# First attention of a two-layer kernel: probabilities transposed by VectorE in 32x32 blocks instead of by TensorE

## The chip, the core and the metric

One Trainium2 chip, one of its NeuronCores. The metric is the device time of one execution in microseconds (us). The five engines are TensorE (PE; its weight loads are PEld), VectorE (DVE), ScalarE (ACT), GpSimd (POOL) and SyncE (SP); they run their own instruction streams and meet only at semaphores.

## The reference

Two layers over x of shape (128, 64, 128), each a cross-attention to a context (128, 64, 96) and a mixture of experts, both with gated residuals. The change is in the first attention alone, 16 heads of width 8, 64 queries and 64 keys per batch entry:

```python
q = (layernorm(x) @ wq + bq)   # 16 heads of 8
k = (ctx @ wk + bk); v = (ctx @ wv + bv)
scores = einsum('bhqd,bhkd->bhqk', q, k) / sqrt(8)
attn = softmax(scores, axis=-1)
out = einsum('bhqk,bhkd->bhqd', attn, v)
x = x + tanh(g_xattn[0]) * (out.reshape(B, S, 128) @ wo + bo)
```

## The kernel before

The kernel is one program of phases that follow each other: constants, first attention (`attention_of_layer0`), first mixture, second attention with routing, second mixture. In the first attention the work unit is a tile of 128 rows, two batch entries of 64; there are 64 tiles, in 16 groups of four. Each engine runs a function `step(t, u, g0)`, with u = t mod 8, in which every operation works on a tile some steps behind: tile t gets its scores, t-1 its maxima subtracted and its exponential, t-2 and t-3 the rest, t-4 the output projection and the update of X. `loop_steps` (lines 45 to 55) writes out the first eight steps, then a loop of eight steps that is run six times with one branch back per turn, then the last twelve. So PE's code for eight steps is one loop body. Nothing schedules but the written order on each engine and the semaphores.

In PE's step: scores of a tile (L619), eight float32 matmuls that contract 32 rows (a batch entry's half of the packed heads) and give 64 queries by 256 (four heads by 64 keys). A float32 matmul appears in the trace as two records. Queries lie on partitions. The row maxima, split in two bfloat16 parts and transposed (L693), are subtracted by a small matmul against `head_cols` (L629), contracting 32 rows for each of the two PSUM banks. The probabilities (`probs`, 128 queries by 16 heads x 64 keys) are transposed on PE in two halves of four 128x128 blocks into one PSUM bank (L646), and ScalarE copies each half to `probsT` (L541). P times V (L675) is 16 matmuls of 128 rows by 32 columns. VectorE sums the denominators (L385), takes reciprocals (L394) and widens them (L406); PE transposes the widened reciprocals (L662) and VectorE multiplies (L419). Line 642 is the output projection. `prepare` makes the next group's normalised rows, keys, queries and values, one of the four kinds per step (L585, L594, L600), through one PSUM bank `prep`; ScalarE copies them out (`evacuate`), VectorE half of the values (`v_odd`, L373); GpSimd spreads the keys over heads (L465).

```python
for s in range(2):
    last = pe.matmul(scores[(u + 1) % 2][:, s, :], rows[bass.ts(s, STRIP), :], c.head_cols[bass.ts(s, STRIP), :],
                     start=False, stop=True, skip_group_check=True)
```

Of the kernel before, what the change touches and what calls it, by code (L numbers as in the profile page):

```python
# [74 lines left out]
def load_constants(nc, sb, psum, sem, c, a, X, dispatch):  # L75
# [15 lines left out]
    c.head_cols_f = sb("head_cols_f", [2 * STRIP, HU * S], F32)  # L91
    c.head_cols = sb("head_cols", [2 * STRIP, HU * S], BF16)
# [38 lines left out]
    c.v_heads = [sb(f"v_heads{i}", [P, GB, HU, STRIP], F32) for i in range(2)]  # L131
    c.parts = sb("parts", [P, P], BF16)
# [13 lines left out]
    def spread(ap, n):  # L146
# [6 lines left out]
        (c.head_of_group[:], a["const_head_of_group"]), (c.head_cols_f[:], a["const_head_cols"]),  # L153
# [28 lines left out]
    with nc.Block() as block:  # L182
# [8 lines left out]
        @block.gpsimd  # L191
        def _(pool):
            pool.memset(c.parts[:], 0.0)
            pool.memset(c.minus_half[:], -0.5)

        @block.scalar
        def _(act):
            act.wait_ge(loads, 16 * len(now))
            act.activation(c.gates[:], c.gates_in[:], ACT.Tanh).then_inc(tanh_done, 1)

        @block.vector
        def _(dve):
# [4 lines left out]
            dve.tensor_copy(c.head_cols[:], c.head_cols_f[:])  # L207
# [55 lines left out]
def attention_of_layer0(nc, sb, psum, sem, c, a, X, dispatch):  # L263
# [14 lines left out]
    neg_max = sb("a_neg_max", [P, H], F32)  # L278


    parts = c.parts
    rows = sb("a_rows", [2 * STRIP, P], BF16)
    probs = [sb(f"a_probs{i}", [P, H * S], F32) for i in range(2)]
    probsT = [sb(f"a_probsT{i}", [P, HU, P], F32) for i in range(2)]
    denom = sb("a_denom", [P, H], F32)
    rec = sb("a_rec", [P, H], F32)
    wide_rec = [sb(f"a_wide_rec{i}", [P, H, DH], F32) for i in range(2)]
    heads_raw = sb("a_heads_raw", [P, P], F32)
    heads_outT = sb("a_heads_outT", [P, P], F32)

    scores = [psum(f"a_scores{i}", [P, 2, 512], F32) for i in range(2)]
    probsT_bank = psum("a_probsT_bank", [P, 512], F32)
    prep = psum("a_prep", [P, 512], F32)
    small = psum("a_small", [P, 512], F32)
    pv = psum("a_pv", [P, 2, P], F32)
    max_parts = parts[:, 0:2 * STRIP].rearrange("p (s a h) -> p s a h", s=2, h=HU)
    max_by_bank = neg_max[:].rearrange("p (s h) -> p s h", s=2)
    y = small[:, 0:D]
    rows_ps = small[:, D:D + P // 2].bitcast(BF16)
# [3 lines left out]
    prep_mm, prep_ev, v_odd_ev = sem("a_prep_mm"), sem("a_prep_ev"), sem("a_v_odd_ev")  # L303
    k_heads_ready = sem("a_k_heads")
    scores_mm, max_done, part1_done, parts_ready = sem("a_scores_mm"), sem("a_max"), sem("a_part1"), sem("a_parts")
# [1479 lines left out]
```

## Time and profile before

| | us |
|---|---|
| median of 3 runs | 1073.1 (1068.34 to 1078.13) |
| the profiled execution | 1074.11 |
| its span, first to last instruction | 1072.3 |
| PE busy | 829.9 (77%) |
| VectorE busy | 680.7 (63%) |
| ScalarE busy | 522.5 (49%) |
| GpSimd busy | 452.0 (42%) |

The first attention takes about the first 334 us of the span. Shares of the whole span mix phases with different limits; the rows below are of the first attention alone.

### The profile page before, as it was taken

Reading aid. Unit: us, or ns where it says so; the run is one execution under the profiler, and the core shown is the slowest. Engines: PE = TensorE matmul, PEld = TensorE weight load, DVE = VectorE, ACT = ScalarE, POOL = GpSimd, SP = SyncE. Lnnn points to the kernel's source line nnn. Section 1 sums busy time; section 2 is a strip of 40 time slices with the busy share of each in tenths; the row PEclk is TensorE's granted clock in tenths of the full one; section 3 lists DMA queues with packets and bytes.
Section 4 is the critical chain, followed back from the end, with each engine's and each line's share of the span. In section 5 each row is a group of like instructions: output and inputs, shape, how many; then the busy total and the mean of one; then the engine's idle time right before and its main releaser. Section 6 shows DMA issues by size and latency. Waiting matters only on the chain. (4 is left out here: it accounts for less than half of the span.)

```text
span 1072.3 us, 25830 instructions
## 1 busy us (share of the span) xinstructions
PE 829.9 (77%) x7905; PEld 607.8 (57%) x7905; DVE 680.7 (63%) x2651; ACT 522.5 (49%) x1115; POOL 452.0 (42%) x454
## 2 busy tenths in 40 slices
PE   2899999999985999996776776763388887887820
PEld 1466666666653566664554554543277776776720
DVE  3688988998895688875855464554244444444435
ACT  1577777777764455543543443442244344433400
POOL 1354544445430111101465655667355555555530
PEclk9999999999997899998966657765699999999965
DMA  4401010100000000002111111111222222222249
GB/s 116 121 20 37 17 34 17 34 17 25 11 2 2 1 0 0 0 2 72 36 48 41 48 40 42 43 38 46 82 76 77 70 73 76 71 70 69 71 154 345
DMA packets 64384, 57.47 MB, mean 54 GB/s; under 512 B 18453, under 2 KB 57901, under 8 KB 64333
## 3 DMA queue, kind: packets, MB, share of 16 engines
q1 hardware_dynamic: 46669, 34.28, 11.1%
q0 software_dynamic: 8640, 17.84, 4.7%
q10 hardware_dynamic: 9024, 4.73, 1.5%
q8 instruction: 25, 0.41, 0.2%
q14 instruction: 26, 0.21, 0.1%
HBM read 32.80 MB, written 24.02 MB: 53 GB/s over the span
## 5 line engine op out<-in xcount | busy, mean ns | idle before, releaser
L1596 POOL DMA_INDIRECT contributions<-d_y,d_token x142 | 135.9, 957 | 135.2 <-DVE d_y L1636 94.0
L1233 POOL DMA_INDIRECT sorted_rows<-r_send,r_slots x128 | 124.7, 974 | 51.4 <-issue 50.6
L1685 PE MATMUL d_u<-d_xT,d_w 128*128 128x256 f32 x284 | 80.6, 409 | 39.2 <-DVE d_xT L1617 21.5
L1656 ACT ACTIVATE d_silu<-d_u 128x512 f32<-128x512 f32 x71 | 42.4, 597 | 139.2 <-PE d_u L1685 88.1
L1617 DVE COPY d_xT<-d_tr 128x256 f32<-128x256 f32 x71 | 30.0, 423 | 120.7 <-PE d_tr L1693 57.5
L465 POOL TENSOR_SCALAR a_k_heads<-a_kT,head_of_group 128x512 f32<-128x512 f32 x60 | 92.9, 1566 | 2.7 <-ACT a_kT L510 2.7
L388 DVE TENSOR_REDUCE a_neg_max<-a_scores 128x16 f32<-128x1024 f32 x64 | 78.2, 1222 | 10.6 <-PE a_scores L619 9.1
L646 PE MATMUL a_probsT_bank<-ident,a_probs 128*128 128x128 f32 x512 | 80.5, 280 | 2.2 <-ACT a_probsT L541 0.3
L541 ACT COPY a_probsT<-a_probsT_bank 128x512 f32<-128x512 f32 x128 | 74.9, 585 | 11.3 <-PE a_probsT_bank L646 11.3
L534 ACT ACTIVATE a_probs<-a_scores 128x1024 f32<-128x1024 f32 x64 | 65.6, 1025 | 28.7 <-PE a_scores L629 28.6
L1685 PEld LDWEIGHTS d_u<-d_xT,d_w 128*128 128x128 f32 x284 | 50.7, 199 | 49.6 <-issue 21.5
L385 DVE TENSOR_REDUCE a_denom<-a_probs 128x16 f32<-128x1024 f32 x64 | 77.3, 1208 | 1.7 <-issue 1.2
L1685 PE MATMUL d_v<-d_xT,d_w 128*128 128x256 f32 x284 | 76.9, 395 | 0.0
L1704 PE MATMUL d_y_bank<-d_w,d_hidden 128*128 128x128 f32 x568 | 75.1, 275 | 0.8 <-DVE d_hidden L1625 0.8
L619 PE MATMUL a_scores<-a_k_heads,a_qT 32*64 32x256 f32 x1024 | 71.7, 395 | 2.8 <-issue 2.6
L1704 PEld LDWEIGHTS d_y_bank<-d_w,d_hidden 128*128 128x128 f32 x568 | 69.1, 192 | 1.1 <-DVE d_hidden L1625 1.0
L646 PEld LDWEIGHTS a_probsT_bank<-ident,a_probs 128*128 128x128 f32 x512 | 56.9, 141 | 17.8 <-issue 11.2
L1636 DVE TENSOR_SCALAR d_y<-d_y_bank,d_rows 128x128 f32<-128x128 f32 x142 | 43.0, 345 | 31.0 <-remote 26.3
L456 POOL TENSOR_TENSOR X<-X,out_bias 128x512 f32 (+1 forms) x16 | 20.6, 1285 | 98.8 <-ACT a_xn L497 98.8
L1685 PEld LDWEIGHTS d_v<-d_xT,d_w 128*128 128x128 f32 x284 | 56.9, 200 | 8.6
L66 POOL TENSOR_SCALAR b_rstd<-b_stats 128x4 f32<-128x4 f32 x16 | 3.7, 228 | 137.5 <-DVE b_stats L752 137.5
L1035 PE MATMUL b_h<-b_xnT,w 128*128 128x512 f32 x96 | 58.3, 694 | 0.0
(208 smaller groups left out, 1915.3 us busy)
## 6 DMA issues: line engine op xcount, KB each, us to landing
d_rows<-sorted_rows SPq DMA_DIRECT2D x71, 130.0 KB
d_pair<-contributions SPq DMA_DIRECT2D x16, 512.0 KB, 7.0
X<-in_x SPq DMA_DIRECT2D x16, 256.0 KB, 3.0
out_x<-X ACTq DMA_DIRECT2D x16, 256.0 KB, 7.4
ctxT<-in_ctx_T SPq DMA_DIRECT2D x16, 192.0 KB, 3.0
c_ctx<-in_ctx SPq DMA_DIRECT2D x16, 192.0 KB
contributions<-d_y,d_token POOLq DMA_INDIRECT x142
w<-in_L_ffn_W SPq DMA_DIRECT2D x2, 1024.0 KB
```

The lines of the kernel that those rows point to most:

```text
L385: dve.reduce_sum(denom[:], probs[u % 2][:].rearrange("p (h k) -> p h k", k=S), AX_X).then_inc(sum_done, 1)
L388: dve.tensor_reduce(neg_max[:], scores[u % 2][:].rearrange("p a (h k) -> p (a h) k", k=S), AX_X, ALU.max, negate=True).then_inc(max_done, 1)
L465: last = pool.tensor_scalar(keys_of_head(par, j), kT[:], c.head_of_group[:, j:j + 1], None, ALU.mult)
L534: act.activation(probs[(u + 1) % 2][:], scores[(u + 1) % 2][:].rearrange("p a n -> p (a n)"), ACT.Exp, scale=SCALE0).then_inc(exp_done, 1)
L541: act.copy(probsT[u % 2][:, half * HU // 2:(half + 1) * HU // 2, :].rearrange("p u q -> p (u q)"), probsT_bank[:]).then_inc(pT_ev, 1)
L619: last = pe.matmul(scores[u % 2][S * b:S * b + S, s, bass.ts(h, 4 * S)], qT[par][rows_in, h, tile, :], k_heads[par][rows_in, tile, h].rear ...
L646: last = pe.transpose(probsT_bank[:, bass.ts(k, P)], probs[u % 2][:, bass.ts(half * HU // 2 + k, P)], c.ident[:])
L1035: pe.matmul(h_bank[(C0 * par + k) % 2][:], c.w1_0[:, 2 * k:2 * k + 2, :].rearrange("d e h -> d (e h)"), xnT[par][:], start=True, stop=True ...
L1233: pool.indirect_dma_start(dispatch.rows, bass.IndirectOffsetOnAxis(ap=slots[par][:, k, j:j + 1], axis=0), send[par][k][:, j, :], None).the ...
L1596: pool.indirect_dma_start(dispatch.contributions, bass.IndirectOffsetOnAxis(ap=token[u % 2][:, h:h + 1], axis=0), shares[u % 2][:, h, :], ...
L1685: last = pe.matmul(bank[q][:, bass.ts(k, TP)], w12[q][:, i * HID1 + k * P:i * HID1 + k * P + P], xT[q][:], start=True, stop=True)
L1704: last = pe.matmul(y[q][:, bass.ts(h, D)], hidden[q][:, k, bass.ts(h, P)], w3[(u + 2) % 4][:, bass.ts(k, D)], start=(k == 0), stop=(k == K ...
```

## The change

Scores are computed so that a partition strip of 32 holds one block of 32 keys' worth of results: a strip is (batch entry, key block j), and within it 32 queries; the free side runs over head, query block i and 32 keys. VectorE then transposes all 32x32 blocks in place with one instruction (`dve.transpose`, 128x1024), and keys lie on partitions. For this the score matmuls become 32 of 32 rows by 32 columns by 128. Maxima: VectorE reduces over each strip of 32 keys, PE transposes that (float32) into the `prep` bank, VectorE takes the minimum over the two key blocks, copies it broadcast as bfloat16 and forms the rest, 32 partitions by 128 each; the subtraction contracts 64 rows for each bank, and `head_cols` is made on the chip from the identity by two ScalarE copies instead of being loaded. P times V becomes 32 matmuls of 64 rows by 32 columns by 64, and 32 more of the same form against ones give the denominators, already in the layout of the outputs. ScalarE takes the reciprocal as exp(-ln(denominator)) and VectorE multiplies. The order of `prepare` becomes keys, rows, queries, values, one per step; a table set with exp and ln is loaded at the start of the phase. Gone are the probability transposes on PE and their copies, the transpose of reciprocals, the denominator sum, the reciprocal, the widening and `v_odd`.

```diff
@@ VectorE's step, in its order @@
+                n = tile_now(t, 3)
+                if n is not None:
+                    dve.wait_ge(rec_step, 2 * n + 2)
...
+                    dve.tensor_tensor(heads_outT[:], rec[:], pv[:, :, 0:S], ALU.mult).then_inc(o_ready, 1)
+                n = tile_now(t, 2)
+                if n is not None:
+                    dve.wait_ge(exp_done, n + 1)
...
+                    dve.transpose(probsT[u % 2][:].rearrange("p h q -> p (h q)"),
+                                  probs[u % 2][:].rearrange("p h i k -> p (h i k)")).then_inc(probsT_ready, 1)
...
+                    dve.tensor_reduce(part_max[:], scores[u % 2][:].rearrange("p s (n k) -> p (s n) k", k=STRIP), AX_X,
+                                      ALU.max, negate=True).then_inc(part_max_done, 1)
...
+                    dve.wait_ge(part_max_mm, n + 1)
+                    dve.tensor_reduce(neg_max[:], part_maxT.rearrange("r (b j q) -> r b q j", b=2, j=2), AX_X,
+                                      ALU.min).then_inc(max_done, 1)
...
+                    dve.tensor_copy(rows[0:STRIP], both).then_inc(high_done, 1)
+                    dve.wait_ge(high_done, n + 1)
+                    dve.tensor_tensor(rows[STRIP:2 * STRIP], both, rows[0:STRIP], ALU.subtract).then_inc(rows_ready, 1)
@@ ScalarE's step @@
+                    act.wait_ge(pv_mm, n + 1)
+                    act.activation(log_denom[:], pv[:, :, S:2 * S], ACT.Ln).then_inc(rec_step, 1)
+                    act.wait_ge(rec_step, 2 * n + 1)
...
+                    act.activation(rec[:], log_denom[:], ACT.Exp, scale=-1.0).then_inc(rec_step, 1)
...
+            act.preload_act_table_set("natural_log_exp_and_others")
+            evacuate(0, 0, KEYS)
@@ PE's step @@
+                        for i in range(2):
+                            for j in range(2):
+                                for s in range(2):
+                                    for b in range(2):
+                                        rows_in = slice(S * b + 32 * s, S * b + 32 * s + 32)
+                                        last = pe.matmul(out[bass.ts(2 * b + j, STRIP), s, h, :, i, :],
+                                                         qT[par][rows_in, h, tile, bass.ts(i, STRIP)],
+                                                         k_heads[par][rows_in, tile, h, :, bass.ts(j, STRIP)],
...
+                        last = pe.matmul(scores[(u + 1) % 2][:, s, :], rows[:].rearrange("r b j q -> r (b j q)"),
+                                         c.head_cols[:, s].rearrange("r n k -> r (n k)"),
...
+                    if not static(t) or t >= 1:
+                        pe.wait_ge(max_done, t)
+                    prepare(g, (u // GT + 1) % 2, u % GT)
...
+                    for j in range(4):
+                        for ones in range(2):
+                            for strip in range(4):
+                                for b in range(2):
+                                    keys = bass.ts(b, S)
+                                    w = (c.ones_heads[keys, j].rearrange("p k w -> p (k w)") if ones else
+                                         c.v_heads[v_par][keys, 4 * tile + strip, bass.ts(j, STRIP)])
+                                    last = pe.matmul(pv[bass.ts(strip, STRIP), b, bass.ts(ones, S)], w,
+                                                     probsT[u % 2][keys, 4 * strip + j, :], start=(j == 0 and ones == 0),
...
+                    pe.wait_ge(part_max_done, t + 1)
+                    g = group_at(g0, 1)
+                    pe.wait_ge(prep_ev, PREP * G if g is None else PREP * g + u % GT + 1)
+                    pe.transpose(part_maxT, part_max[:], c.ident[:]).then_inc(part_max_mm, 1)
```

## Rows read from the trace of the kernel before

**Rows 1.** The table of stages: one turn of the loop, eight tiles
```profile
104.80:141.50 36.70, 35.87 (x601) 23.84 (x600) 33.04 (x86) 27.94 (x63) 17.47 (x14) 1.00 0.08 25
```

**Rows 2.** Instructions of line 51, the loops: PE's branch, first and last start
```profile
L51 PEldq COMPARE_BRANCH  x6: 76/208/233, 104.8 to 288.3; - x6
```

**Rows 3.** Timeline of PE, one tile: start, duration, line, operation, names, shapes, count
```profile
201.92 1.09 PE L619 MATMUL a_scores<-a_k_heads,a_qT 32*64 32x256 f32 x16
202.94 0.39 PE L629 MATMUL a_scores<-head_cols,a_rows 32*128 32x512 bf16 x2
203.26 0.49 PE L642 MATMUL a_small<-wo,a_heads_outT 128*128 128x128 f32 x2
203.59 0.60 PE L646 MATMUL a_probsT_bank<-ident,a_probs 128*128 128x128 f32 x4
204.02 0.27 PE L662 MATMUL a_pv<-ident,a_wide_rec 128*128 128x128 f32 x1
204.23 0.65 PE L675 MATMUL a_pv<-a_probsT,v_heads 128*32 128x64 f32 x32
204.81 1.08 PE L594 MATMUL a_prep<-a_xnT,wq 128*64 128x256 f32 x8
205.83 0.66 PE L646 MATMUL a_probsT_bank<-ident,a_probs 128*128 128x128 f32 x4
206.32 0.22 PE L693 MATMUL a_small<-ident_bf,parts 128*128 128x128 bf16 x1
206.47 1.09 PE L619 MATMUL a_scores<-a_k_heads,a_qT 32*64 32x256 f32 x16
```

**Rows 4.** Groups by line, 104.8 to 288.3 us, forty tiles
```profile
L385 DVE TENSOR_REDUCE a_denom<-a_probs 128x16 f32<-128x1024 f32 x41 | 49.5, 1208 | 1.5 <-issue 1.2
L388 DVE TENSOR_REDUCE a_neg_max<-a_scores 128x16 f32<-128x1024 f32 x40 | 48.9, 1222 | 5.2 <-PE a_scores L619 4.3
L541 ACT COPY a_probsT<-a_probsT_bank 128x512 f32<-128x512 f32 x81 | 47.4, 586 | 5.4 <-PE a_probsT_bank L646 5.4
...
L406 DVE COPY a_wide_rec<-a_rec 128x128 f32<-128x128 f32 x40 | 11.9, 298 | 0.1
...
L565 ACT COPY a_rows<-a_small 64x128 bf16<-64x128 bf16 x40 | 10.4, 261 | 0.0
...
L399 DVE CAST parts<-a_neg_max 128x16 bf16<-128x16 f32 x40 | 10.4, 259 | 0.0
...
L394 DVE RECIPROCAL a_rec<-a_denom 128x16 f32<-128x16 f32 x40 | 9.7, 243 | 0.0
...
L373 DVE COPY v_heads<-a_prep 64x256 f32<-64x256 f32 x20 | 7.7, 424 | 4.7 <-PE a_prep L600 4.7
L401 DVE TENSOR_TENSOR parts<-a_neg_max,parts 128x16 bf16<-128x16 f32 x40 | 7.0, 175 | 1.4
```

**Rows 5.** Timeline of VectorE, a step with layer statistics
```profile
54.43 0.86 DVE L355 BATCH_NORM_STATS2 a_stats<-X 128x6 f32<-128x128 f32 x4
...
55.70 1.19 DVE L385 TENSOR_REDUCE a_denom<-a_probs 128x16 f32<-128x1024 f32 x1
```

**Rows 6.** Timeline of all engines, the front of the attention
```profile
0.71 1.28 ACT L199 ACT_TABLE_LOAD   x1 [0.58 <-PEq L1769]
...
25.44 1.67 DVE L440 TENSOR_SCALAR a_k_heads<-a_kT,head_of_group 128x512 f32<-128x512 f32 x4 [3.28 <-ACT a_kT L510]
...
25.46 1.98 PE L594 MATMUL a_prep<-a_xnT,wq 128*64 128x256 f32 x8 [0.94 <-ACT a_kT L510]
...
30.28 1.98 PE L619 MATMUL a_scores<-a_k_heads,a_qT 32*64 32x256 f32 x16
```

**Rows 7.** DMA queues, 68.1 to 104.8 us: packets, MB, share of 16 engines
```profile
q8 instruction: 5, 0.08, 1.0%
```

**Rows 8.** DMA queues and issues, 141.5 to 288 us; no instruction queue listed
```profile
q1 hardware_dynamic: 4480, 3.21, 7.1%
...
X<-in_x SPq DMA_DIRECT2D x7, 256.0 KB, 3.0
```

More of the change, by code:

```diff
@@ L192, in _ @@
         def _(pool):
-            pool.memset(c.parts[:], 0.0)
+            for j in range(4):
+                for k in range(4):
+                    pool.memset(c.ones_heads[:, j, k, :], float(j == k))
             pool.memset(c.minus_half[:], -0.5)
@@ L199, in _ @@
             act.activation(c.gates[:], c.gates_in[:], ACT.Tanh).then_inc(tanh_done, 1)
+            for part in range(2):
+                diagonal = c.ident[bass.ts(part, STRIP), bass.ts(part, STRIP)]
+                act.copy(c.head_cols[bass.ts(part, STRIP)].rearrange("p s n k -> p (s n) k"),
+                         diagonal.unsqueeze(2).broadcast_to([STRIP, STRIP, STRIP]))
         @block.vector
@@ L366, in offset @@
                                          op0=ALU.mult, op1=ALU.mult).then_inc(offset_ready, 1)
-            def v_odd(g, par):
-                dve.wait_ge(prep_mm, PREP * g + 4)
-                if not static(g) or g >= 2:
-                    dve.wait_ge(pv_mm, GT * (g - 1))
-                for u in range(2):
-                    last = dve.tensor_copy(*values_of_pairs(par, slice(S, P), u, DH))
-                last.then_inc(v_odd_ev, 1)
             def step(t, u, g0):
@@ L522, in evacuate @@
                         act.wait_ge(pv_mm, GT * (g - 1))
-                    for u in range(2):
-                        last = act.copy(*values_of_pairs(par, slice(0, S), u, 0))
-                    last.then_inc(prep_ev, 1)
+                    last = act.copy(c.v_heads[par][:].rearrange("p n (j w) -> p n j w", j=4)[:, :, :, 0:DH],
+                                    prep[:].rearrange("p (n j w) -> p n j w", j=4, w=DH))
+                last.then_inc(prep_ev, 1)
             def step(t, u, g0):
@@ L637, in step @@
                     pe.wait_ge(o_ready, n + 1)
-                    pe.wait_ge(rows_ready, min(t, TILES) if static(t) else t)
                     if not static(n) or n >= 1:
                         pe.wait_ge(x_updated, n)
-                    pe.matmul(y, heads_outT[:], c.wo0[:], start=True, stop=True).then_inc(y_mm, 1)
-                def transpose_probs(half):
-                    for k in range(HU // 2):
-                        last = pe.transpose(probsT_bank[:, bass.ts(k, P)],
-                                            probs[u % 2][:, bass.ts(half * HU // 2 + k, P)], c.ident[:])
-                    last.then_inc(pT_mm, 1)
+                    pe.matmul(y, heads_outT[:].rearrange("p b q -> p (b q)"), c.wo0[:], start=True, stop=True).then_inc(y_mm, 1)
@@ L679, in step @@
[L679 to L693 removed]
+                    wait_alone(pe, probsT_ready, n + 1)
```

258 lines of the change are left out of this document (75 added, 183 removed).

## The prediction

> **What bounds the kernel now.** I read the table of stages first: from 104.8 to 141.5 us the span is one turn of the first attention's loop, eight tiles, and PE is busy for 35.87 of 36.70 us, VectorE for 33.04, ScalarE for 27.94 [rows 1]. So PE sets the pace and VectorE, with 10% to spare, is next. The loop branch gives the period: six takes from 104.8 to 288.3 us are five turns, 36.70 us each, 4.587 us for a tile [rows 2]. The timeline of PE over one tile shows that nothing else ends its waits: each group of matmuls starts where the one before stops issuing [rows 3]. Differences of starts are the price of a group on PE: scores 1.02, maximum subtraction 0.32, output projection 0.33, four probability transposes 0.43, spreading the reciprocals 0.21, P times V 0.58, one projection 1.02, four more transposes 0.49, maxima 0.15; together 4.55. Only a change in this sum, or a VectorE loop that grows past it, moves the time.
>
> [...]
>
> **PE, part by part.** Added and removed per tile:
> - Scores become 32 matmuls of 32 rows by 32 columns, 128 columns wide: 64 records. Row strip and column strip differ for all eight of (j, s, b). If eight run side by side: 8 waves x 0.108 + 0.16 = 1.02, unchanged. If only four, as everywhere in the trace: 16 x 0.108 + 0.16 = 1.89.
> - P times V takes 64 matmuls with 64 rows (values, and ones for the denominators), 128 records. With eight lanes 16 x 0.055 + 0.16 = 1.05, with four 1.92, against 0.58.
> - The subtraction now contracts 64 rows, so its two 512-column matmuls follow each other: 2 x 0.215 + 0.11 = 0.54 against 0.32.
> - Both groups of probability transposes (0.92) and the reciprocal transpose (0.21) go.
> - Projections: keys and queries 1.02 each, rows about 0.46 (a transpose costs 0.11 in its group of four), values 8 records x 0.108 + 0.1 = 0.97: mean 0.87. Projection output 0.33, maxima 0.20.
>
> Sum with eight lanes: 1.02 + 0.54 + 0.33 + 0.87 + 1.05 + 0.20 = 4.01. No row shows row and column strips combined, so the bounds are 4.01 and 5.76; I take eight lanes, because the trace shows four by rows (scores) and four by columns (P times V) and the operands of the new forms never share a strip pair. [...]
>
> **VectorE.** It loses the denominator sum 1.21, reciprocal 0.24, cast 0.26, difference 0.18, widening 0.30 and its half of the values, 7.7 us over 40 tiles or 0.19: 2.38 [rows 4]. It gains the block transpose of 1024 elements, a second reduction of 128 elements from PSUM and two 128-element operations on the maxima. [...] The small ones I take at about 0.3 each, as the widening. Busy: 4.13 - 2.38 + 1.2 + 0.9 = 3.85 a tile. But this work now stands in a ring: PE transposes the maxima, some 0.38 later (a transpose of 0.27 and the semaphore) VectorE reduces (0.30), copies (0.25), subtracts (0.25), multiplies the head outputs (0.25), transposes (1.13 start to start, like 55.70 to the next reduction), reduces the next scores (1.22), and 0.06 later PE may transpose again: 3.84. One tile in four also carries the layer statistics, 1.27 from 54.43 to 55.70 [rows 5], of which some 0.3 fits into the waiting for PE: about 4.8 in that step. The X update (0.2) fits into the wait.
>
> **Both together.** PE's own steps are about 4.2, 3.65, 4.2, 4.1 and the maxima reach the subtraction about 1.2 after PE's transpose, where 1.2 of PE work (transpose, scores) covers them, with 0.1 to 0.2 uncovered. Taking in each step what ends last, and the statistics pushing into the step behind them: 4.2, 4.6, 4.2, 4.1, mean 4.27. If each small VectorE operation is 0.05 longer, 4.4; if each is 0.05 shorter, 4.13. ScalarE loses 1.17 of copies of transposed probabilities, 0.26 of maxima rows and the copy of the raw heads, gains a logarithm and an exponential of 128 elements, 0.6 with the wait between them: far below 4.27, beside other work [rows 4]. If that cover went, its reciprocal would hold the head product at the start of VectorE's step. Saved: 0.32 x 55 tiles (the last ones have no projections: PE's 4.55 less some 0.9 is below VectorE's ring, and nothing is won) = 17.4 us.
>
> **The front.** Keys are projected ahead of the normalised rows, while ScalarE is idle. Then the values' projection starts where the queries' did, 25.46, and scores at about 27.4 instead of 30.28 [rows 6]: -3 us. The extra table load costs ScalarE 1.28 [rows 6] at a time when it waits anyway; its two copies of 1024 elements end with VectorE's set-up, within 0.3 us. One constant load less gives that back.
>
> **Code.** Here the change adds something that the kernel never had to pay. PE's loop was 600 matmuls and 600 weight loads a turn [rows 1], and in its first turn five 16 KB packets of instructions came in, 240 instructions each; from 141.5 to 288 us the transfers list no instruction queue at all [rows 7, 8]: the body stayed. The new body is 204 matmuls and as many loads a tile, with waits about 3,400 instructions, thirteen packets. If it also stays, it costs nothing after the first turn. If not, each of the five returns waits for a packet: its transfer is 1.0% of 16 engines over 36.7 us through 5, 1.2 us, with some start 1.6; a load of data lands after 3.0 [rows 8]. Five times 1.6 is 8 us, five times 3.0 is 15. I take 8, the instruction packet's own row. A burst of P times V eats a packet's worth in 1.05 us, less than its transfer; PE's slack against VectorE covers most of that, 0 to 0.3 us a tile; I take 0.05, 3 us.
>
> [...]
>
> **Sum.** 1074.1 (span 1072.3 and 1.8 around it) - 17.4 - 3 + 8 + 3 = 1064.7; the median of the runs lies 1.0 below the profiled one: about 1063.
>
> **Rivals.**
> 1. Slower: the instruction stream binds. If the next packet is asked for only when the one before is entered, and takes as long to land as a data load, a tile of 1.65 packets cannot be shorter than 1.65 x 3.0 = 4.95 us. Against 4.587 that is +0.36 x 60 = 22, with five returns at 3.0 (+15) and the front (-3): about 1108. It decides from 2.8 us a packet on. For it: one packet at a time, evenly spaced, in the first turn. Against it: transfers of 1.2 us. Chance 0.25.
> 2. Four lanes only: PE 5.76 a tile, +1.17 x 60 - 3 + 8 = about 1145. Chance 0.10.
> 3. VectorE becomes the bound: a transpose in two passes makes the ring 5.0 us, about 1100; small operations longer by 0.05 to 0.1 leave 4.4 to 4.5, 1070 to 1075. Or ScalarE reloads a table for each change between logarithm and exponential: 2.6 us a tile, beside 2.8 of work, 5.4, about 1120. Together 0.10.
> 4. The body stays resident and the bursts cost nothing: 1053. Chance 0.10.
> The forecast keeps 0.45, spread over 1050 to 1076 by the small terms.
>
> **From cases to numbers.** 1% is 10.7 us and about what a measurement of this kernel can tell from no change. Faster by more: rival 4 and rather more than half of the forecast's own spread, 0.38. Slower by more: rivals 1 and 2, most of 3, a little of the forecast: 0.36. Between: 0.26. The range runs from 1047 to 1112: it holds the forecast, rivals 1 and 4, and most of 3, and leaves out four lanes and the tails. The forecast's own range is 1050 to 1076.
>
> **What the changed profile would show.** The new loop branch period by eight: 4.27 plus returns. Scores and P times V at 1.0 and 1.05 start to start, or 1.9 each for four lanes. The block transpose at 1.2. Instruction packets: about thirteen in every turn if the body does not stay, and a hole in PE of 1.5 to 3 us behind each taken branch; holes of PE inside P times V that end with no semaphore speak for rival 1. PE waiting for the maxima's rows more than 0.3 us in each tile would say that VectorE's ring, not PE, is the bound. I would be wrong most likely in code supply or in the small VectorE operations of the ring.

## The result, and where the time went

The changed kernel takes 1326.6 us in the median (1324.0 to 1329.9) against 1071.1 for the kernel before on the same chip: 1.2375 times as long, 95% interval 1.2319 to 1.2431. The forecast was 1063, in a range of 1047 to 1112. The profiled execution of the changed kernel, first lines of its page, its DMA queue of instructions, and the branch of TensorE's loop:

```profile
span 1322.1 us, 41801 instructions
...
PE 926.9 (70%) x16161; PEld 673.2 (51%) x16161; DVE 665.8 (50%) x2554; ACT 474.5 (36%) x975; POOL 453.2 (34%) x469
...
q8 instruction: 124, 2.03, 0.7%
...
L51 PEldq COMPARE_BRANCH  x6: 83/4848/5064, 151.4 to 505.3; - x6
```

The branch row is the one to set beside [rows 2]. Five turns take 353.9 us, so a turn is 70.8 us and a tile 8.85, where it was 4.587; and a taken branch, 0.208 us before, takes 4.85 us. The loss has three parts that add up to the difference of the spans, 249.8: up to the first branch at tile 16, 46.6 us (151.4 against 104.8); in the five turns, 170.4 us (353.9 against 183.5); behind the last branch, 32.8 us (816.8 against 784.0).

One turn, as the table of stages has it (busy us and instructions of each engine, granted clock, DMA share, GB/s), answers to [rows 1]; below it the instruction queue over the two turns from 151.4 to 293.0 us, for [rows 7, 8]:

```profile
151.40:222.18 70.78, 47.97 (x1595) 32.36 (x1594) 30.64 (x74) 21.52 (x44) 17.62 (x14) 0.79 0.06 16
...
q8 instruction: 30, 0.49, 1.5%
```

No engine is busy for its turn: PE 68%, VectorE 43%. In the kernel before, PE was busy for 98% and no instruction packet came in this stretch; now fifteen come in every turn, one per 4.72 us in the mean, and the granted clock is 0.79 (and 0.73 in the turn after this one) where it was 1.00.

What ends the idle time of VectorE (first row) and of PE (the others): the line that waits, what released it, us in total, times, longest; 151.4 to 505.3 us:

```profile
DVE a_heads_outT L367 <- PE a_y L589: 128.5, 40, 8.2
...
PEld a_pv L611 <- issue: 76.2, 55, 4.0
...
PEld a_scores L570 <- issue: 59.4, 37, 5.6
PE a_scores L570 <- issue: 49.7, 24, 5.4
```

"issue" means that no semaphore ended the wait. The timeline of PE shows such a hole in the middle of a burst of value matmuls, whose operands all lay ready (only groups of several records are kept here, PE is silent from 202.6 to 204.58; answers to [rows 3]):

```profile
201.19 0.32 PE L611 MATMUL a_pv<-a_probsT,v_heads 64*32 64x64 f32 x13 [1.22 <-DVE a_probsT L373]
...
202.32 0.29 PE L611 MATMUL a_pv<-a_probsT,ones_heads 64*32 64x64 f32 x6
204.58 0.31 PE L611 MATMUL a_pv<-a_probsT,ones_heads 64*32 64x64 f32 x6 [1.97 <-issue]
204.82 0.28 PE L619 MATMUL a_prep<-ident,a_part_max 128*32 128x128 f32 x1
```

That is the picture that the prediction gave to its first rival. But the first row of this timeline holds a second thing: the burst itself began 1.22 us late, for VectorE's transposition. VectorE's new operations have about the durations that were forecast (groups by line, for [rows 4]):

```profile
L373 DVE STREAM_TRANSPOSE a_probsT<-a_probs 128x1024 f32<-128x1024 f32 x40 | 49.5, 1238 | 0.0
L380 DVE TENSOR_REDUCE a_part_max<-a_scores 128x32 f32<-128x1024 f32 x40 | 47.4, 1184 | 0.0
...
L404 DVE TENSOR_TENSOR a_rows<-a_neg_max,a_rows 32x128 bf16<-32x128 f32 x40 | 11.2, 281 | 1.4
L396 DVE TENSOR_REDUCE a_neg_max<-a_prep 32x64 f32<-32x128 f32 x40 | 11.0, 276 | 65.2 <-PE a_prep L619 64.8
L402 DVE CAST a_rows<-a_neg_max 32x128 bf16<-32x128 f32 x40 | 9.4, 236 | 4.7 <-DVE a_neg_max L396 1.1
```

### The profile page after: what moved, and what is told of

The parts are those of the page before. It is cut to its first block and busy times, and to the rows that moved or that the text cites. A ratio compares the mean times of both kernels' runs of the same rounds, so it can differ in the third digit from the quotient of the medians.

```text
span 1322.1 us, 41801 instructions
## 1 busy us (share of the span) xinstructions
PE 926.9 (70%) x16161; PEld 673.2 (51%) x16161; DVE 665.8 (50%) x2554; ACT 474.5 (36%) x975; POOL 453.2 (34%) x469
## 5 line engine op out<-in xcount | busy, mean ns | idle before, releaser
L1522 POOL DMA_INDIRECT contributions<-d_y,d_token x142 | 135.9, 957 | 132.6 <-DVE d_y L1562 89.1
L570 PE MATMUL a_scores<-a_k_heads,a_qT 32*32 32x128 f32 x4096 | 106.3, 332 | 61.4 <-issue 61.4
L611 PE MATMUL a_pv<-a_probsT,v_heads 64*32 64x64 f32 x4096 | 103.3, 262 | 55.5 <-DVE a_probsT L373 31.6
L611 PE MATMUL a_pv<-a_probsT,ones_heads 64*32 64x64 f32 x4096 | 107.8, 261 | 40.8 <-issue 40.8
L611 PEld LDWEIGHTS a_pv<-a_probsT,v_heads 64*32 64x32 f32 x4096 | 83.0, 120 | 81.9 <-issue 81.8
L570 PEld LDWEIGHTS a_scores<-a_k_heads,a_qT 32*32 32x32 f32 x4096 | 76.0, 125 | 81.1 <-issue 76.8
L367 DVE TENSOR_TENSOR a_heads_outT<-a_rec,a_pv 128x128 f32<-128x128 f32 x64 | 18.4, 288 | 185.5 <-PE a_y L589 185.5
L611 PEld LDWEIGHTS a_pv<-a_probsT,ones_heads 64*32 64x32 f32 x4096 | 80.3, 124 | 44.1 <-issue 44.0
L373 DVE STREAM_TRANSPOSE a_probsT<-a_probs 128x1024 f32<-128x1024 f32 x64 | 79.2, 1238 | 0.0
L380 DVE TENSOR_REDUCE a_part_max<-a_scores 128x32 f32<-128x1024 f32 x64 | 75.9, 1186 | 5.6 <-PE a_scores L570 5.6
L513 ACT ACTIVATE a_log_denom<-a_pv 128x128 f32<-128x128 f32 x64 | 17.7, 277 | 168.6 <-PE a_pv L611 168.6
```

The costliest lines, as they stand in the source:

```text
L373: dve.transpose(probsT[u % 2][:].rearrange("p h q -> p (h q)"), probs[u % 2][:].rearrange("p h i k -> p (h i k)")).then_inc(probsT_ready, 1)
L380: dve.tensor_reduce(part_max[:], scores[u % 2][:].rearrange("p s (n k) -> p (s n) k", k=STRIP), AX_X, ALU.max, negate=True).then_inc(part_ ...
L570: last = pe.matmul(out[bass.ts(2 * b + j, STRIP), s, h, :, i, :], qT[par][rows_in, h, tile, bass.ts(i, STRIP)], k_heads[par][rows_in, tile ...
L611: last = pe.matmul(pv[bass.ts(strip, STRIP), b, bass.ts(ones, S)], w, probsT[u % 2][keys, 4 * strip + j, :], start=(j == 0 and ones == 0), ...
L1522: pool.indirect_dma_start(dispatch.contributions, bass.IndirectOffsetOnAxis(ap=token[u % 2][:, h:h + 1], axis=0), shares[u % 2][:, h, :], ...
```

## The experiments

The theory: TensorE waits for its own instructions, because its loop, 3327 instruction words where it was 1281, no longer stays resident. (Words are counted in the compiled programs; 25 packets with 0.41 MB in the page of before are 16.4 KB each, and five of them came for the 1281 words of before's first turn [rows 7]: 256 words each, called a unit below.) The rivals: VectorE's ring, small matmuls that are slow by themselves, and a clock that falls of its own. All but one of the sets ran on chips where the kernel before takes 974 to 977 us in the median; there the later stages are shorter (680.5 us behind the last branch against 784.0), the first attention is the same (below, the run of the kernel before). Only the set with three of the four-step kernels (called head, head in bfloat16 and cast below) ran where it takes 1070. So ratios, and times per tile in the loop, are what to compare. Branch rows read: shortest, median and longest in ns, start of the first and the last.

**1. The kernel before with smaller matmuls.** The same columns stream in more instructions, in some or all of the eight unrolled steps (u < 2: quarter, u < 4: half, always: full):

```diff
-  pe.matmul(scores[...][.., s, bass.ts(h, 4 * S)], qT[...], k_heads[...], start=(h == 0), ...)
+  for j in range(4):
+      pe.matmul(scores[...][.., s, bass.ts(4 * h + j, S)], qT[...], k_heads[...][:, bass.ts(j, S)], start=(h == 0 and j == 0), ...)
-  pe.matmul(pv[bass.ts(strip, STRIP), 0, bass.ts(b, S)], v, probsT[...][:, k, bass.ts(b, S)], ...)
+  for i in range(2):
+      pe.matmul(pv[..., bass.ts(2 * b + i, S // 2)], v, probsT[...][:, k, bass.ts(2 * b + i, S // 2)], ...)
```

Half: 

> The kernel before, with TensorE's work cut into smaller instructions and nothing else changed: in four of the eight unrolled steps each score matmul of 256 columns becomes four of 64 and each value matmul of 64 columns becomes two of 32. The same columns stream. TensorE's loop body grows from 1281 to 1921 instruction words (7.5 units of 256, which is the 16 KB of one q8 packet). Theory (instruction supply, with a body that no longer stays resident as the cause): 1921 words still stay resident, no q8 packets between the first turns and the end of the loop, the branch at about 0.2 us as in the kernel before, and the loop at 4.6 to 4.9 us per tile: 1073 to 1090 us. Rival (small matmuls are slow by themselves, by their count): 80 more matmuls per four steps each cost a fixed 0.05 to 0.1 us, so 1 to 2 us per changed tile, 25 to 60 us over the kernel, 1100 to 1135 us.

Full: 

> As the run before it, in all eight unrolled steps: a loop body of 2561 words, 10 units. Theory (supply): the body no longer stays; q8 packets run through the whole loop, about 10 per turn, each taken branch takes about 4.8 us instead of 0.2, and every unit crossed costs up to 1 to 3 us where the work between is short; a turn takes about ten packets at 4.7 us = 47 us = 5.9 us per tile against 4.6, so about 1.3 x 55 = 70 us more: 1120 to 1170 us, with a jump far over twice what the half edit costs. Rival (fixed cost of small matmuls): just twice the loss of the half edit, the branch still 0.2 us, no q8 packets in the loop.

Quarter: 

> The kernel before with its score and value matmuls cut small in two of the eight unrolled steps: a body of 1601 words, where 1921 no longer stayed resident and the 1665 of the four-step kernel did. Theory (a threshold of size): resident, branch 0.2 us, no q8 packets in the loop, and a turn of 36.7 us plus two times what a changed step costs TensorE in work, 0.5 to 1.5 us each: 37.5 to 40 us per turn. Rival (the loss of the half edit, 14.4 us per turn for four steps, was mostly the small matmuls themselves): half of that, 7 us per turn: 43 to 44 us.

Measured: 1012.4, 1067.5 and 1128.6 us. The branches of quarter, half and full:

```profile
L51 PEldq COMPARE_BRANCH  x6: 76/210/245, 111.8 to 321.9; - x6
```
```profile
L51 PEldq COMPARE_BRANCH  x6: 79/3720/3848, 126.8 to 382.2; - x6
```
```profile
L51 PEldq COMPARE_BRANCH  x6: 79/3677/3876, 139.3 to 428.8; - x6
```

A turn takes 42.0, 51.1 and 57.9 us (36.7 unedited). Residence is lost between 1601 and 1921 words, earlier than I had expected (I took 1921 for safe), and a lost branch costs 3.7 us. The rival was right about the size of the rest, though: two changed steps cost 5.3 us with a resident loop, 2.66 each, where I had allowed 0.5 to 1.5. From quarter to half, two more steps and the branch (5.3 + 3.5) give 8.8 of the 9.1 measured; from half to full 6.8, less than the four steps alone would. So cutting matmuls small in the form of the kernel before is dear by itself, and this test does not isolate the supply. Nor is all of the 2.66 the matmuls' own: PE was busy for 98% of the five turns of quarter, yet the granted clock was between 0.92 and 1.00 in them. In a changed step at full clock (205.51 to 211.85 us) the scores take 2.62 start to start for 1.02 and the values 0.79 for 0.58, so 1.8 us more.

**2. No loop at all.** TensorE's loop of the changed kernel is written out.

```diff
-            loop_steps(pe, 2 * GT, TILES // (2 * GT) - 2, LAST, step)
+            for t in range(LAST):
+                step(t, t % (2 * GT), t // GT)
```

> The changed kernel with TensorE's loop over tiles written out: the same instructions in the same order, no branch in the first attention, 26,400 words once through. Theory A (each unit of 256 words arrives about 4.7 us after the one before is entered, and the taken branches are a small part of it): the branches' five times 4.85 us go, the rest stays: 8.2 to 8.9 us per tile, 1290 to 1330 us. Theory B (the loss is in the branches and in what is fetched anew after them; straight code is fetched far enough ahead): about 4.3 to 5.5 us per tile, 1060 to 1150 us.

Measured: 1195.7 us, against 1234.0 for the changed kernel on this kind of chip (run below): 38 less. By the branches of ScalarE, which kept its loop, a tile takes 8.03 us (six takes, 152.8 to 474.0 us) for 8.91. Five taken branches at 4.79 us are 24 of it; 14 stay unexplained. (The forecast's 1290 to 1330 was made for the first kind of chip; less 93, its theory A gives 1197 to 1237.) From 150 to 300 us 30 packets came and PE was busy for 111.3 of 150 us. So most of the loss needs no branch: straight code waits too.

The changed kernel and the kernel before, run again: 

> The changed kernel, unchanged, for a trace and a time on this kind of chip, where the later stages take 97 us less. Expected: the loop at 8.85 us per tile as in its first trace (70.8 us per turn, branch 4.85 us), and 1322 less some 95 us: 1215 to 1240 us.

> The kernel before, unchanged, for a trace on the chip of the experiments, where its median is 974 us against 1071 us on the chip of the first comparison. Expected: the first attention as in its first trace (36.7 us per turn of the loop of eight tiles, branch 0.2 us, granted clock 1.00), and the 97 us less in the later stages, at a higher granted clock there.

Measured 1234.0 and 970.8 us. The branch rows come out nearly as on the first chip, 4.59 and 8.91 us a tile for 4.59 and 8.85 (before_again first):

```profile
L51 PEldq COMPARE_BRANCH  x6: 76/208/233, 104.9 to 288.4; - x6
```
```profile
L51 PEldq COMPARE_BRANCH  x6: 79/4789/4973, 155.5 to 511.8; - x6
```

**3. A loop half as long.** TensorE's loop is unrolled by four steps. In this kernel the stationary operands of TensorE's matmuls have fixed addresses in the loop body, which a body of four steps can't switch between two buffers, so GpSimd brings each tile's operands into buffers with a place per tile of the group, and SyncE loads the context once for the keys and once for the values:

```diff
+            def copy_queries(t, u, g):          # on GpSimd, two tiles ahead; copy_values is alike
+                wait_alone(pool, prep_ev, PREP * g + QUERIES + 1)
+                wait_alone(pool, scores_mm, t - 3)
+                pool.tensor_tensor(k_tile[:, u % GT], kT[...] (broadcast over heads), head_of_group (broadcast), ALU.mult)
+                pool.tensor_copy(q_tile[:, :, u % GT], qT[...][:, :, u % GT]).then_inc(q_tile_ready, 1)
-            loop_steps(pe, 2 * GT, TILES // (2 * GT) - 2, LAST, step)
+            loop_steps(pe, 2 * GT, TILES // GT - 4, LAST, step, GT)      # period 4
```

> The changed kernel with TensorE's loop unrolled by four steps instead of eight, 1665 words instead of 3327, so that it can stay resident. [...] TensorE's stream, VectorE's ring with the transposition and ScalarE's work are those of the changed kernel. Theory (supply): no q8 packets during the loop, the branch at about 0.2 us, granted clock near 1.0, about 4.3 us per tile (up to 4.8 where VectorE's ring ends last) against 8.85: 1050 to 1090 us. Rival 1 (the transposition on VectorE, in the ring exp, transposition, values, is what binds): still above 7 us per tile, over 1230 us. Rival 2 (eight-lane small matmuls stream slowly or hold the clock down by themselves): the granted clock stays at 0.6 to 0.8 and the tile above 6.5 us, over 1200 us. Rival 3 (GpSimd, with about 1.6 us more per tile, binds): its busy share near all of the loop, 5 us or more per tile.

Measured: 1176.2 us, 1.207 times before (1.204 to 1.211), where the changed kernel stands at 1234.0/975.3 = 1.265. The branch and two waits (129.5 to 449.5, and 130 to 449 us):

```profile
L48 PEldq COMPARE_BRANCH  x12: 76/208/242, 129.5 to 449.5; - x12
```
```profile
PE a_scores L586 <- POOL a_q_tile L453: 48.6, 11, 4.4
PE a_pv L626 <- DVE a_probsT L384: 34.0, 33, 1.4
```

The loop is resident, and still a tile takes 320.0/44 = 7.27 us: the theory alone is not enough. The two rows say what else there is. The first wait is my copies', held behind GpSimd's addition of the bias, which waits for ScalarE's normalisation (175.3 us, 11 times, at most 22.4). The second belongs to the changed kernel: VectorE's order.

**4. GpSimd's bias moved, and then VectorE's order.**

```diff
-                if u % GT == 1: ... add_bias(group_at(g0, 2))     # GpSimd
+                if u % GT == 0: ... add_bias(group_at(g0, 1))
```
```diff
 # VectorE's step (four_steps_order and after_order)
+                transpose probsT of tile t-2        # waits for exp_done, long there
                 heads_outT of tile t-3              # waits for y_mm of tile t-4: TensorE, behind scores and subtraction
-                transpose probsT of tile t-2
                 part_max of tile t
```

> The four-step kernel with one GpSimd operation moved: the addition of the output bias to X, which waited in GpSimd's second step of a group for ScalarE's normalisation of its fourth, and held the copies behind it, is done one step group later. In the run before it TensorE idled 4.25 us per turn of four tiles for the copies. Theory (that idle time is an artefact of my copies): 1.06 us per tile less, 7.27 to about 6.2 us per tile, about 65 us less, 1110 us. Rival (the time is then lost to the ring through VectorE, or to the clock): the tile stays above 6.8 us.

> The run before it, and VectorE's transposition of tile t-2 put ahead of its product for tile t-3, which waits for the output projection of tile t-4 on TensorE, behind scores and subtraction. Theory (VectorE's order makes TensorE wait 0.95 to 1.4 us per tile before each burst of values, by the rows DVE a_probsT): that hole goes, about 1.0 us per tile less, 5.0 to 5.3 us per tile, granted clock up, 1030 to 1060 us. Rival (the ring exp, transposition, values only turns into another wait, as VectorE has the same work): the tile stays within 0.3 us of the run before.

> The changed kernel with that exchange on VectorE alone, TensorE's loop still 3327 words. Theory (with the code arriving in units, the supply sets the pace, and VectorE's wait is hidden in it): at most 0.3 us per tile off 8.85, 1200 to 1235 us on this chip. Rival (the VectorE wait adds to the supply's stalls): about 1 us per tile, 65 us less than the changed kernel would need here (about 1230), so 1165 us.

Measured, in this order: 1103.6 us; 1022.5 (1.048 times before, 1.045 to 1.051); 1146.4. The branches, in that order:

```profile
L48 PEldq COMPARE_BRANCH  x12: 76/208/242, 119.1 to 381.3; - x12
```
```profile
L48 PEldq COMPARE_BRANCH  x12: 76/208/242, 112.5 to 318.0; - x12
```
```profile
L51 PEldq COMPARE_BRANCH  x6: 79/4872/5087, 138.3 to 439.4; - x6
```

Per tile: 5.96, 4.67 and 7.53 us. This makes a square. VectorE's order is worth 8.85 - 7.53 = 1.32 in the long loop and 5.96 - 4.67 = 1.29 in the resident one; the resident loop (with GpSimd's copies and their bias) is worth 2.89 with the old order and 2.86 with the new. (With the 8.91 of after_again, on the same kind of chip, 1.38 and 2.95.) Two causes that add, and my theory that the supply would hide VectorE's wait was wrong: nothing pays for the other.

No experiment held the clock fixed, but the traces say how much of the time can be its share. The whole loop of the changed kernel, and a turn of four tiles of four_steps_bias, resident and with VectorE's old order:

```profile
151.40:505.30 353.90, 245.21 (x8162) 163.32 (x8161) 154.30 (x370) 108.15 (x221) 87.90 (x70) 0.77 0.05 15
```
```profile
131.00:154.80 23.80, 18.69 (x826) 13.29 (x818) 15.82 (x37) 10.87 (x23) 8.64 (x15) 1.00 0.09 28
```

Divided by tiles, over whole loops, PE's time is busy and idle: 6.13 + 2.72 us in the changed kernel (granted clock 0.77), 5.67 + 1.86 in after_order (0.83), 4.68 + 1.27 in four_steps_bias (0.98), 4.56 + 0.11 in four_steps_order (1.00). The matmuls are nearly the same in all four, so the longer busy time is an estimate of what the lower clock costs: 1.57 of the 4.18 us between the first and the last. The two values of the order agree less than they seem to: in the long loop 0.46 of its 1.32 us is shorter busy time at a higher clock, in the resident loop 0.13 of 1.29.

A turn of four tiles of four_steps_order; then PE's timeline, groups of the values left out but one:

```profile
131.20:149.90 18.70, 18.25 (x825) 13.12 (x816) 15.81 (x37) 10.79 (x22) 8.85 (x16) 1.00 0.11 35
```
```profile
218.67 0.34 PE L624 MATMUL a_pv<-a_probsT,v_heads 64*32 64x64 f32 x16
...
220.09 0.28 PE L632 MATMUL a_prep<-ident,a_part_max 128*32 128x128 f32 x1
220.30 1.15 PE L584 MATMUL a_scores<-a_k_tile,a_q_tile 32*32 32x128 f32 x64
221.39 0.60 PE L594 MATMUL a_scores<-head_cols,a_rows 64*128 64x512 bf16 x2
221.92 0.49 PE L603 MATMUL a_y<-wo,a_heads_outT 128*128 128x128 f32 x2
222.24 1.06 PE L566 MATMUL a_prep<-wv,ctx_values 96*128 96x128 f32 x8
```

PE is busy for 98% again and is the bound; VectorE has 15.81 of 18.70. Start to start: values and ones 1.42, maxima 0.21, scores 1.09, subtraction 0.53, output projection 0.32.

**5. Straight code, and where the loop lies.** A tile in the cured loop costs 4.67 us, nearly before's 4.587, yet the kernel is 4.8% slower. Of the 55.7 us between the two profiled executions (1024.6 and 968.9) the loop makes 3.7. Behind the last branch, at tile 56 in both, lie 26 more than in before_again (706.6 against 680.5), and ahead of tile 12 about as many (112.5 against 104.9 less four tiles): the straight steps. Two edits turn straight steps into turns of the loop, at the end and at the start:

```diff
-            loop_steps(pe, 2 * GT, TILES // GT - 4, LAST, step, GT)
+            loop_steps(pe, 2 * GT, TILES // GT - 3, LAST, step, GT)      # four_steps_tail: tiles 8 to 59
+            loop_steps(pe, GT, TILES // GT - 2, LAST, step, GT)          # four_steps_head: tiles 4 to 59
```

> The four-step kernel with VectorE's new order, its loop on TensorE run one turn further (to tile 59 instead of 55), so that 1656 words of straight code at the end go. Its straight code before and after the loop costs more per tile than the loop: after the last branch the run took 26 us more than the kernel before does after its own. Theory (straight code waits for its instructions, a resident loop doesn't): 4 tiles at 4.67 us instead of about 7, and a higher clock: 6 to 12 us less than 1022.5, so 1010 to 1017 us. Rival (the last tiles are slow because the pipeline drains and other engines have their constants to do): within 3 us of 1022.5.

> The four-step float32 kernel with the longer tail, its loop on TensorE begun at tile 4 instead of 8, so that 1655 words of straight code ahead of it go (a semaphore is raised by one at the start so that no wait is on zero). Theory (straight code of small matmuls waits for its instructions at about 6.5 us or more a tile, the resident loop takes 4.67): 4 tiles times about 2 us, 7 to 12 us less than 1018.7: 1006 to 1012 us. Rival (the start is slow for other reasons: loads, the filling pipeline): within 3 us of 1018.7.

Measured: tail 1018.7 us, 1.046 (1.040 to 1.051) times before; beside 1.048 that decides nothing. Head: 1337.3 us against 1069.8, 1.252 (1.244 to 1.259). Four steps fewer of straight code, the same loop of 1665 words, and a quarter more time. Branches and one turn of head:

```profile
L48 PEldq COMPARE_BRANCH  x13: 76/208/237, 114.2 to 338.3; - x13
```
```profile
L48 PEldq COMPARE_BRANCH  x14: 76/5072/5422, 87.6 to 566.5; - x14
```
```profile
161.30:198.10 36.80, 25.34 (x738) 16.29 (x741) 17.22 (x36) 10.42 (x22) 7.30 (x14) 0.68 0.06 16
```

9.21 us a tile in the place of 4.67, at a granted clock of 0.68 in this turn and 0.75 over the loop: neither the number of words in the loop nor the work in it can be the cause, for both are the same. I counted where each loop lies in the compiled program:

```
kernel                  first word  words  units touched  branch us  us per tile
bf16                        2090     1153        5          0.21        4.58
before                      1115     1281        6          0.21        4.59
head bf16, cast              947     1153        6          0.21        4.59, 4.61
quarter                     1307     1601        7          0.21        5.25
four steps, bias, order, tail  2858  1665        7          0.21   7.27, 5.96, 4.67, 4.67
half                        1563     1921        8          3.72        6.39
head                        1203     1665        8          5.07        9.21
full                        2203     2561       11          3.68        7.24
after, after_order          2855     3327       14          4.85        8.85, 7.53
```

Every loop that touches seven units or fewer stays, every one that touches eight or more doesn't. And those that don't stay fetch one unit more per turn than they touch: nine for eight (27 packets in three turns of head, and of half), twelve for eleven (full), fifteen for fourteen (the changed kernel). If seven is the limit, 120 words that do nothing, anywhere ahead of the loop, must cure head and break tail:

```diff
+            pool.memset(c.minus_half[:], -0.5).then_inc(early, 1)     # GpSimd's first operation
+            for _ in range(120):                                     # TensorE, ahead of its first wait for loads
+                wait_alone(pe, early, 1)
             pe.wait_ge(loads, 16 * len(now))
```

> The kernel whose loop begins at tile 4, and 120 words that do nothing (no-operations behind a wait that is long met) at the start of TensorE's program, while it waits for the first loads. Nothing else. The loop's 1665 words then begin at word 43 of a unit of 256 instead of word 179 and touch 7 units instead of 8. Theory (a loop stays resident if it touches no more than 7 units): the branch at 0.2 us, no q8 packets in the loop, 4.67 us per tile instead of 9.2, and 4 tiles of straight code fewer than in the kernel with the longer tail (1.0456 of before): 1.035 to 1.042 of before. Rival (the loop's start at tile 4, or the wait that I added to it, makes it slow): 1.25 of before again.

> The kernel with the longer tail, which had 4.67 us per tile and 1.0456 of before, and the same 120 idle words at the start of TensorE's program. Its loop of 1665 words then begins at word 162 of a unit instead of word 42 and touches 8 units instead of 7. Theory: the loop falls out of residence: branch about 5 us, about 9 us per tile, 1.25 to 1.27 of before. Rival: unchanged, 1.04 to 1.05 of before.

Measured: head with the idle words 1009.4 us, 1.034 (1.028 to 1.041) times before; tail with them 1144.0, 1.175 (1.166 to 1.183). Branches, first head_pad, then tail_pad:

```profile
L48 PEldq COMPARE_BRANCH  x14: 76/208/240, 83.7 to 326.4; - x14
```
```profile
L48 PEldq COMPARE_BRANCH  x13: 79/234/5101, 113.1 to 455.8; - x13
```

4.67 and 7.14 us a tile; from 151 to 305 us 22 packets came in tail_pad, none in order, tail and head_pad between 130 and 300. So position decides. Half right in size only: in tail_pad the median branch is 0.23 us and the longest 5.1, so only some of its branches lose their target, and a tile takes less than the 9 us that I expected. Its packets come nine at a time, within some 34 us (197.4 to 231.3 us), and then none for 23 to 26 us. In head_pad PE's busy and idle time per tile are 4.56 + 0.11 us at a granted clock of 1.00, in head 6.23 + 2.98 at 0.75. Why head (word 179 of a unit) does worse than tail_pad (word 162) wasn't tried. Head_pad also gives a price of the straight steps: 1.034 against tail's 1.046, some 11 us for four, though the two intervals touch.

**6. What comes next if TensorE's share shrinks.** Probabilities, values and ones become bfloat16 (they are rounded; the sums stay in float32), in the kernel with the longer tail; then also the loop begins at tile 4, then VectorE's CAST is replaced by an operation with the same result:

```diff
-    probs, probsT, v_group, v_heads, ones_heads: F32
+    probs, probsT, v_group, v_heads, ones_heads: BF16
```
```diff
-                    dve.tensor_copy(rows[0:STRIP], both).then_inc(high_done, 1)
+                    dve.tensor_tensor(rows[0:STRIP], both, both, ALU.max).then_inc(high_done, 1)     # four_steps_cast
```

> The run before it with probabilities, values and the ones in bfloat16 (the sums stay in float32 in PSUM; the probabilities are rounded to 8 bits). [...] Theory (TensorE's work and words are what is left above VectorE's 4.1 us): 4.1 to 4.3 us per tile, 20 to 25 us less in the loop and 8 to 15 us less in the straight parts: 970 to 990 us. Rival (another engine or the ring binds by then): the tile stays above 4.5 us, over 1000 us.

> The same in bfloat16 (1143 words fewer ahead of the loop). Theory: 3 to 7 us less than 984.6, so 978 to 982 us. Rival: within 2 us of 984.6.

> The run before it, with VectorE's CAST of the maxima into rows replaced by a TENSOR_TENSOR (the larger of the value and itself) with the same result. The CAST took 461 ns in the mean in bfloat16, 214 at least and up to 848 where GpSimd works beside it; the TENSOR_TENSOR behind it took 280 to 283 always. Theory (VectorE sets the tile at 4.58, and CAST waits for GpSimd): 0.15 to 0.2 us per tile less, 7 to 11 us off: 968 to 973 us. Rival (the ring through TensorE, ScalarE and VectorE is a latency in which the CAST's wait is only part of the slack, or GpSimd's work meets other VectorE operations instead): within 2 us of the run before.

Measured against before: 1.011 (1.007 to 1.015), 1.011 (1.005 to 1.017), 1.010 (1.006 to 1.015). The first run's 984.6 us lie in the theory's 970 to 990, but a tile takes 4.58 us (4.59 and 4.61 in the other two) and not 4.1 to 4.3, so the rival was right about the loop: in four_steps_bf16 PE is busy for only 125.9 of 150 us (150 to 300), and VectorE for 135.9. PE now waits for the maxima's rows (in this stretch the weight load of the subtraction 17.8 us, its matmul 9.0), and the first operation that makes them is long (view of the tile a_rows, 130 to 280 us: shortest, median, longest in ns; first the CAST in four_steps_bf16, then its replacement in four_steps_cast):

```profile
L413 DVE CAST a_rows<-a_neg_max x32: 214/424/848, 132.6 to 275.7; 32x128 bf16<-32x128 f32 x32
```
```profile
L413 DVE TENSOR_TENSOR a_rows<-a_neg_max x32: 279/488/912, 132.8 to 275.4; 32x128 bf16<-32x128 f32 x32
```

The replacement stretches as much as the CAST did, so it isn't the kind of operation; what it meets is open. (In four_steps_order, where GpSimd makes the same copies, its median is 226 ns and its longest 370.) No version here beats the kernel before.

## Why the prediction was wrong, step by step

- **PE bounds the kernel before, and how many small matmuls run side by side**: right. Scores 1.09 for a forecast 1.02, subtraction 0.53 for 0.54, output projection 0.32 for 0.33, maxima 0.21 for 0.20. How many run side by side is an estimate: a record of 128 columns over the whole array takes 0.108, from the four transposes in 0.43 of [rows 3]; at that price before's 16 score records of 256 columns in 1.02 are about 3.4 at a time, and the 64 of 128 columns, 1.72 four at a time, took 1.09. So more than four at a time: rival 2 falls. No run shows the 0.16 us that the terms of scores and values hold beside their waves; the runs show the whole bursts. Values and ones took 1.42 for 1.05, the one term of this sum that was badly mis-sized; projections took 0.92 in the mean of their four kinds for 0.87. The sum is 4.49, not 4.01, and short waits make it 4.67. (The total for rival 2 was added up about 4 us low: 1074.1 + 70.2 - 3 + 8 is 1149.)
- **VectorE's operations**: right. The 1.2 for the transposition was the author's estimate, and 1.238 was measured. Measured too: the reduction 1.184, the small ones 0.24 to 0.29.
- **VectorE's ring**: failed in one step. It counted the product of the head outputs at 0.25 and let the transposition follow it at once. But that product waits for the output projection of tile t-4, which stands on PE behind the scores and the subtraction (128.5 us of waiting in 40 tiles), and the transposition is queued behind it, and PE's burst of values behind that. The exchange on VectorE measured it twice: 1.32 and 1.29 us a tile. The prediction counted durations in the ring and not what each operation in it waits for.
- **Both together, 4.27 a tile**: 4.67 once both causes are gone, against 4.587. Even cured, the change has nothing to win in the loop: the forecast 17.4 us rested on the 1.05 of the values' burst above all.
- **Code**: the step that failed most, and the one named as likeliest to. It took 1.6 us for a return and 0.05 us a tile for bursts; measured are 4.85 us for a taken branch, and for residence lost 2.9 us per tile in all, of which up to half is longer busy time at the lower clock. It also knew no price for straight code, where 46.6 us were lost ahead of the first branch and 32.8 behind the last one, against a forecast of 3 us won at the front.
- **Rival 1** came nearest, with a chance of 0.25: instruction packets in every turn, and holes in PE's bursts that no semaphore ends. That one unit is asked for at a time was not shown; the rival's size came from a data load's 3.0 us for a packet. Its count was near, fifteen packets a turn for the forecast thirteen. But no fixed interval replaces its 3.0 us: the mean was 4.72 us in the changed kernel, 4.0 in after_order with the same fifteen (60.2 us a turn), and 4.8 in the full edit of the kernel before, where PE was still busy for 92% of the loop. The mean interval contains the work and the other waits, so it can't be put into the rival's formula as a price. That the trace of before had 1.2 us transfers was the row that misled: PE stood idle for 1.97 us in mid-burst, and 4.85 at a branch.
- **Residence**: the prediction left open whether a body of thirteen packets stays, and rival 4, in which it does, falls. The loops that touch eight units and more have branches of 3.7 to 5.1 us in the median (tail_pad 0.23, its longest 5.1) against 0.21, with seven units the loop stayed. Why one packet more came per turn than units touched was not shown.
- **Clock**: the prediction had no term for it. The granted clock, 0.68 to 0.87 in the turns of the changed kernel, after_order and head, is at 1.00 in four_steps_order, with nearly the same matmuls. It didn't go by PE's busy share alone: four_steps_bias had 0.98 with PE busy for 79% of its loop, and before_small_quarter 0.92 to 1.00 with 98%. Its share of the 4.2 us a tile is about 1.6 by the estimate of experiment 4; no run held it fixed.

## What to carry to other kernels

Count TensorE's instructions as you count its columns. A change that trades few large matmuls for many small ones (408 matmul and weight-load records a tile here for 150) has a bill in instruction supply: find out from the queue of instruction packets and from the branch whether the loop is resident, and if it is near the edge, look at where it begins too, since 120 idle words took the kernel from 1.252 to 1.034 of before in one place and from 1.046 to 1.175 in another. When an operation is moved to another engine, write down what stands ahead of it in that engine's queue and what that waits for; a duration alone says nothing about when it ends.

## What the runs showed of the hardware

- The loops on TensorE that touched up to seven units of 256 instruction words stayed resident, and those that touched eight or more did not, 1665 words in both cases: 4.67 us a tile in tail and head_pad (seven) against 9.21 in head and 7.14 in tail_pad (eight). That the position of a loop could matter so much I had not expected.
- Code that isn't resident made TensorE wait in straight code too, not only at taken branches: 30 packets came in 150 us in the unrolled kernel and PE was busy for 111 of them. A branch back to code that had not stayed took 3.7 to 5.1 us in the median (half, full, the changed kernel, head; in tail_pad, where some of the branches lost their target, 0.23), one to resident code 0.21. Packets came one per 4.0 to 5.7 us in the mean (after_order, half), which is no fixed pace, while a load of 256 KB landed in 3.0 (3.1 in the unrolled kernel).
- The loops that weren't resident fetched one unit more per turn than they touched: nine for eight (half, head), twelve for eleven (full), fifteen for fourteen (the changed kernel). In tail_pad, which touches eight, packets came in only some of the turns, nine at a time.
- A matmul cut into smaller ones cost more than its columns: 2.66 us for a step with 40 more matmuls in the form of the kernel before, the loop resident (1.8 at a granted clock of 1.00), while the form of the changed kernel, 32 rows by 32 columns, ran 64 score records in 1.09 us.
- VectorE's transposition of 128x1024 in 32x32 blocks took 1.24 us in float32 (the changed kernel) and 1.245 in bfloat16 (four_steps_bf16): half the bytes brought nothing.
